# Six of sixteen row-block pairs of a feed-forward product done with seven block products in place of eight

## The chip, the cores and the metric

One core of a Trainium2 chip runs one program. The metric is the device time in microseconds, the median of several executions. The kernel before takes 1193.26 us.

## The reference

The input x has 4 x 1024 rows of 1024 numbers: 32 blocks ("tiles") of 128 rows. Three stages follow one another; each adds to x. The change touches the first.

```python
def ffn(x):                       # stages 1 and 3; x is the layer-normed input
    dots = softmax(x @ centroids.T / 0.1)          # 64 clusters
    hits = dots > 0.01
    dense = x @ weight.T + bias                    # weight 1024 x 1024
    return where(any(hits, axis=1)[:, None] & any(hits, axis=0)[assignments][None, :], dense, 0)
x = x + 0.5 * ffn(layernorm(x))
x = x + attention(layernorm(x))   # projections of q, k, v; attention over the 32 channels of a head
x = x + 0.5 * ffn(layernorm(x))
```

## The kernel before

All is float32. A product is made from three: each operand is split into a rounded high part and the rest (`w_hi`, `w_lo`; `even_hi`, `even_lo` for even pairs and `odd_hi`, `odd_lo` for odd pairs), and `product` (line 280) runs, for each of 8 blocks of the contraction, hi x hi, hi x lo and lo x hi into one bank of 512 columns: 24 matmuls. W is transposed and split at the start, in 16 steps (`transpose_rows`, `high_rows`, `low_rows`).

The first stage goes over the tiles in pairs p = 0 to 15 (tiles 2p and 2p+1). A tile t goes through these steps, each on its own engine:

- SP loads x (`load_first`, line 396, three buffers `xa`), VectorE takes mean and variance (`stats_first`), Pool makes the factors (`factors_first`, line 628), ScalarE the normed rows (`norm_first`, line 742).
- From tile 4 on, SP stores the normed rows (`store_normed`) and loads them back with their 32 x 32 blocks in transposed places, as four transfers (`load_blocks`, line 410); VectorE turns each block (`turn_first`, line 984). Tiles 0 to 3 are turned by TensorE.
- ScalarE rounds the high part (`high_first`, line 751), VectorE subtracts for the low part (`low_first`, line 988). TensorE needs both.
- TensorE makes two products a tile, one for each half of the columns (`product_first(t, h)`, line 1273), and for each pair the cluster logits (`pair_first`, line 1293), which ScalarE copies (`copy_pair`, line 763) and TensorE turns (`fold_pair`, line 1302); VectorE and ScalarE make the softmax from them.
- VectorE adds the bias and moves a half from its bank to `f_out` (`read_first`, line 1000). A bank is free for its next product when this is done. Pool clears the rows not selected (`select_tokens`, line 631), SP stores `f_out[t % 2]` (`store_first`, line 425).

Beside it the projection weights are prepared, a block of 128 rows a pair from p = 1 on: SP loads `proj_raw` (`load_proj`), Pool sums heads (`sum_heads`), ScalarE moves k and v and rounds (`move_kv`, `high_proj`), Pool subtracts (`low_proj`).

Every engine runs its instructions strictly in the order in which they are written; a wait on a semaphore holds all that stands behind it. The orders are written by hand: lines 458 to 482 for SP's queue, 657 to 673 for Pool, 801 to 816 for ScalarE, 1057 to 1069 for VectorE and 1338 to 1347 for TensorE. There a pair is products (2p, 0) and (2p, 1), the logits of pair p+1, then (2p+1, 0) and (2p+1, 1); each product takes the bank that the product of the same half two tiles ago had:

```python
for p in range(1, NP - 2):
    product_first(2 * p, 0, {3 if p == 1 else 1: lambda: fold_pair(p)})
    product_first(2 * p, 1)
    if p > 1:
        pair_first(p + 1)
    product_first(2 * p + 1, 0)
```

## Time and profile before

| what | value |
|---|---|
| median of three runs | 1193.26 us (1192.64 to 1194.24) |
| the profiled execution, its own time | 1196.15 us |
| its span in the trace | 1194.3 us |
| busy: TensorE / VectorE / ScalarE / Pool | 1181.7 / 799.3 / 499.2 / 441.0 us |
| first stage, within the span | 0 to about 387 us |

Busy time is the time in which an engine had an instruction at work; a matmul's recorded length overlaps the next one's, so that the distance between starts tells the rate. The first stage is a third of the span. The durations below are those of this one execution.

### The profile page before, as it was taken

Reading aid. Unit: us, or ns where it says so; the run is one execution under the profiler, and the core shown is the slowest. Engines: PE = TensorE matmul, PEld = TensorE weight load, DVE = VectorE, ACT = ScalarE, POOL = GpSimd, SP = SyncE. Lnnn points to the kernel's source line nnn. Section 1 sums busy time; section 2 is a strip of 40 time slices with the busy share of each in tenths; the row PEclk is TensorE's granted clock in tenths of the full one; section 3 lists DMA queues with packets and bytes.
Section 4 is the critical chain, followed back from the end, with each engine's and each line's share of the span. In section 5 each row is a group of like instructions: output and inputs, shape, how many; then the busy total and the mean of one; then the engine's idle time right before and its main releaser. Section 6 shows DMA issues by size and latency. Waiting matters only on the chain.

```text
span 1194.3 us, 24986 instructions
## 1 busy us (share of the span) xinstructions
PE 1181.7 (99%) x10072; PEld 1002.5 (84%) x10072; DVE 799.3 (67%) x1272; ACT 499.2 (42%) x718; POOL 441.0 (37%) x582
## 2 busy tenths in 40 slices
PE   7999999999999999999999999999999999999998
PEld 6888888888888888888888888888888878888887
DVE  6654554455444477787777877778777774199987
ACT  5232233222211355656656656565565663211110
POOL 1335445543424643433434334344343210051332
PEclk9999999999999999999999999999999999999999
DMA  8578777876565366565565666565655565017885
GB/s 275 144 206 232 207 206 193 225 211 182 164 189 159 98 169 169 148 171 146 160 166 139 181 152 152 160 155 164 161 142 164 129 169 193 2 72 259 279 304 195
DMA packets 344978, 208.73 MB, mean 175 GB/s; under 512 B 289440, under 2 KB 308640, under 8 KB 344864
## 3 DMA queue, kind: packets, MB, share of 16 engines
q1 hardware_dynamic: 329696, 187.73, 56.2%
q10 hardware_dynamic: 15168, 19.40, 4.7%
q8 instruction: 80, 1.31, 0.5%
q14 instruction: 34, 0.28, 0.1%
HBM read 118.49 MB, written 88.60 MB: 173 GB/s over the span
## 4 chain that ended last, share of the span: by engine, by line
PE 91%; DMA 3%; DVE 2%; issue 1%; ACT 1%; SPq 1%; POOL 1%; POOLq 0%; DVEq 0%
PE ps_b L285 9%; PE ps_q L285 8%; PE ps_q L287 8%; PE ps_q L286 8%; PE ps_b L287 8%; PE ps_b L286 8%; PE ps_a L285 8%; PE ps_a L287 8%; PE ps_a L286 8%; PE ps_t L292 6%; PE ps_q L1450 3%; PE ps_q L299 2%; PE ps_q L301 2%; PE ps_q L1425 2%; DMA y_scratch<-xa 1%
## 5 line engine op out<-in xcount | busy, mean ns | idle before, releaser
L318 POOL TENSOR_TENSOR var_eps<-moments,eps 128x1 f32<-128x1 f32 x96 | 18.2, 190 | 396.6 <-DVE moments L314 396.6
L285 PE MATMUL ps_a<-w_hi,odd_hi 128*128 128x512 f32 x368 | 147.7, 401 | 0.0
L287 PE MATMUL ps_a<-w_hi,odd_lo 128*128 128x512 f32 x368 | 143.8, 391 | 0.0
L286 PE MATMUL ps_a<-w_lo,odd_hi 128*128 128x512 f32 x368 | 143.2, 389 | 0.0
L635 POOL TENSOR_SCALAR f_out<-f_out,token_on 128x1024 f32<-128x1024 f32 x30 | 85.6, 2852 | 75.6 <-DVE f_out L1013 75.3
L686 POOL TENSOR_TENSOR x_ring<-x_ring,f_tmp 128x1024 f32<-128x1024 f32 x32 | 77.3, 2414 | 91.2 <-DVE best L1159 58.5
L285 PE MATMUL ps_b<-proj_hi,y_hi 128*128 128x512 f32 x256 | 103.3, 403 | 0.0
L287 PE MATMUL ps_b<-proj_hi,y_lo 128*128 128x512 f32 x256 | 100.0, 391 | 0.0
L286 PE MATMUL ps_b<-proj_lo,y_hi 128*128 128x512 f32 x256 | 99.7, 390 | 0.0
L327 ACT ACTIVATE y_tok<-x_ring,norms 128x1024 f32<-128x1024 f32 x64 | 79.7, 1245 | 38.0 <-ACT o_head L881 21.0
L737 POOL TENSOR_TENSOR late<-late,mask 128x1024 f32<-128x1024 f32 x18 | 44.1, 2463 | 137.3 <-DMA late<-x_scratch 91.6
L1120 DVE TENSOR_TENSOR y_lo<-ps_t,y_hi 128x1024 fp32r<-128x1024 f32 x32 | 39.2, 1224 | 76.1 <-ACT y_hi L900 76.1
L893 ACT COPY v_diag<-part 32x256 f32<-32x256 f32 x128 | 82.7, 646 | 1.1
L287 PEld LDWEIGHTS ps_a<-w_hi,odd_lo 128*128 128x128 f32 x368 | 69.1, 188 | 15.1
L286 PEld LDWEIGHTS ps_a<-w_lo,odd_hi 128*128 128x128 f32 x368 | 69.3, 188 | 13.1
L285 PEld LDWEIGHTS ps_a<-w_hi,odd_hi 128*128 128x128 f32 x368 | 69.2, 188 | 12.7
L285 PE MATMUL ps_q<-w_hi,odd_hi 128*128 128x512 f32 (+1 forms) x208 | 79.5, 382 | 0.0
L287 PE MATMUL ps_q<-w_hi,odd_lo 128*128 128x512 f32 (+1 forms) x208 | 79.3, 381 | 0.0
L286 PE MATMUL ps_q<-w_lo,odd_hi 128*128 128x512 f32 (+1 forms) x208 | 79.3, 381 | 0.0
L285 PE MATMUL ps_q<-proj_hi,y_hi 128*128 128x256 f32 x256 | 74.8, 292 | 0.0
L287 PE MATMUL ps_q<-proj_hi,y_lo 128*128 128x256 f32 x256 | 72.5, 283 | 0.0
L286 PE MATMUL ps_q<-proj_lo,y_hi 128*128 128x256 f32 x256 | 72.4, 283 | 0.0
(219 smaller groups left out, 3113.1 us busy)
## 6 DMA issues: line engine op xcount, KB each, us to landing
xa<-in_L_attn_x SPq DMA_DIRECT2D x32, 512.0 KB, 5.0
f_tmp<-f_scratch SPq DMA_DIRECT2D x32, 512.0 KB, 4.2
x_ring<-in_L_attn_x SPq DMA_DIRECT2D x32, 512.0 KB, 3.6
f_scratch<-f_out SPq DMA_DIRECT2D x30, 512.0 KB, 4.0
x_scratch<-x_ring SPq DMA_DIRECT2D x30, 512.0 KB, 3.5
y_scratch<-xa SPq DMA_DIRECT2D x28, 512.0 KB, 4.6
ya_tok<-y_scratch SPq DMA_DIRECT2D x112, 128.0 KB, 3.3
late<-x_scratch SPq DMA_DIRECT2D x22, 512.0 KB, 6.7
```

What stands on the lines that cost most here:

```text
L285: pe.matmul(acc, hi[:, k, :], w_h[:, k, cols], start=(k == 0), stop=False)
L286: pe.matmul(acc, hi[:, k, :], w_l[:, k, cols], start=False, stop=False)
L287: last = pe.matmul(acc, lo[:, k, :], w_h[:, k, cols], start=False, stop=(k == KB - 1))
L292: last = pe.transpose(ps_t[:, k, :], src[:, k * P:(k + 1) * P], ident[:, :])
L299: last = pe.matmul(pair_ps, cen[:, k, :], hi[:, k, :, :], start=(k == 0), stop=(k == KB - 1))
L327: return act.activation(y, x, ACT.Identity, bias=norms[of][:, t, 0:1], scale=norms[of][:, t, 1:2])
L635: pool.tensor_scalar(f_out[t % 2][:, :], f_out[t % 2][:, :], token_on[0][:, t:t + 1], None, ALU.mult).then_inc(f1_on, 1)
L686: pool.tensor_tensor(x_ring[t % RING][:, :], x_ring[t % RING][:, :], f_tmp[:, :], ALU.add).then_inc(x1, 1)
L737: pool.tensor_tensor(f[:, :], f[:, :], mask[:, :], ALU.mult).then_inc(s_masked, 1)
L893: last = act.copy(v_diag[rows, :].rearrange("p (k q g c) -> p q k g c", k=R4, g=HKV, c=T4)[:, :, :, :, c], v_cols[rows, :].rearrange("p (q ...
L1120: dve.tensor_tensor(y2_lo[:, :, :], ps_t[:, :, :], y2_hi[:, :, :].bitcast(F32), ALU.subtract).then_inc(lo2, 1)
L1450: last = pe.matmul(scores_of[32 * c:32 * c + 32, r, :, j, :], q_head[rows, n * D:(n + 1) * D], k_mask[rows, n * P:(n + 1) * P].rearrange(" ...
```

## The change

Pairs 4 to 9 (`SEVEN`) are computed with seven products of half the contraction (12 matmuls each) in place of eight such halves. The operands are cut in two by rows (the two tiles of the pair), by contraction and by columns. Pool makes four sums of the input's blocks in place (`sum_blocks`), ScalarE and VectorE split them (`high_sum`, `low_sum`) into `odd_hi` and `odd_lo`; all six pairs have their own input in `even_hi` and `even_lo`. VectorE combines the seven results by eight reads; Pool adds the difference of the two bias halves (`bias_first`). The selection of these tiles moves from Pool to ScalarE (`select_first`).

Four combinations of W's blocks are made once, during pairs 1 to 3, through one buffer `t_sum`: VectorE sums (3, 3, 2 and 2 instructions of 2048 columns, in `blocks_three`, `blocks_one`, `blocks_two`, `blocks_four`), ScalarE rounds, Pool subtracts (the last one VectorE). Three go to `t_hi` and `t_lo`, the fourth over a quarter of W, which is stored in memory before and loaded back after the last pair. `t_sum` lies where the odd pairs' normed rows go later (`ya_more`), and `t_hi`, `t_lo` where the projection weights go: these are now prepared from pair 10 on, two blocks a pair. Pair 3 has its products by halves of the columns. Some semaphores that are done by then are used again under new names (`t_step`, `t_hi_set`, `t_lo_set`, `block_step`, `seven_done`). The core of the diff:

```diff
+SA, SB = 4, 10
...
+t_hi = middle.enter_context(nc.sbuf_tensor("t_hi", [P, 3, QB, HALF], F32R))
+t_lo = middle.enter_context(nc.sbuf_tensor("t_lo", [P, 3, QB, HALF], F32R))
...
         if t - 2 < BY_PE:
             sp.wait_ge(t1, t - 1)
+        elif p == SA + 1:
+            sp.wait_ge(t_lo_set, 5)
+        elif SA + 1 < p <= SB:
+            sp.wait_ge(lo1, t - 3)
+            sp.wait_ge(sum_lo, parts_count(p - 2, 4))
         else:
             sp.wait_ge(lo1, t - 1)
+        if SA < p <= SB:
+            sp.wait_ge(y_in[t % 2], 64 * ((t - BY_PE) // 2))
...
-        sp.wait_ge(f1_on, t + 1)
+        sp.wait_ge(f1_on, t + 2 - 2 * (t % 2) if t // 2 in SEVEN else t + 1)
...
         if p > 0:
             store_first(2 * p - 1)
+        if p - 1 in SEVEN:
+            store_first(2 * p - 2)
+        if p > SB:
+            load_next_proj(2 * (p - SB) - 1)
+        if p == NP - 2:
+            load_next_proj(KB)
         if 2 * p + 5 < LAST:
             load_first(2 * p + 5)
         if 2 * p + 4 < NT:
             load_first(2 * p + 6)
         if p == NP - 2:
             load_attention()
-        store_first(2 * p)
+        if p not in SEVEN:
+            store_first(2 * p)
         if 2 * p + 5 < LAST:
             store_normed(2 * p + 5)
         if 2 * p + 7 == LAST:
             load_first(LAST)
-        if 1 <= p <= KB:
-            load_proj(p - 1, [w[(p - 1) * P:p * P].rearrange("p d h -> p (d h)") for w in (Wq, Wk, Wv)])
-        if p == KB + 1:
-            load_proj(KB, [b.rearrange("d h -> (d h)").partition_broadcast(P) for b in (bq, bk, bv)])
+        if SB <= p < NP - 2:
+            load_next_proj(2 * (p - SB))
         if 2 * p + 5 < NT:
             load_blocks(2 * p + 5)
+        if p == 1:
+            sp.wait_ge(wt_lo, 2 * KB)
+            for n, w in enumerate((w_hi, w_lo)):
+                sp.dma_start(w_d[n], upper(w)[:, :, half(1)].bitcast(F32)).then_inc(w_saved, 16)
+        if p == SB - 1:
+            sp.wait_ge(seven_done, seven_count(p, 1))
+            for n, w in enumerate((w_hi, w_lo)):
+                sp.dma_start(upper(w)[:, :, half(1)].bitcast(F32), w_d[n]).then_inc(w_back, 16)
...
+    def low_block(m):
+        n = T_ORDER[m]
+        pool.wait_ge(t_hi_set, m + 2)
+        pool.tensor_tensor(t_lo[:, n], t_sum[:, :, :], t_hi[:, n].bitcast(F32),
+                           ALU.subtract).then_inc(t_lo_set, 1)
+    def sum_blocks(p):
+        top, bottom = first_turned(2 * p), first_turned(2 * p + 1)
+        pool.wait_ge(lo1, 2 * p + 2)
+        pool.tensor_tensor(lower(bottom), upper(bottom), lower(bottom), ALU.add).then_inc(sum_set, 1)
+        pool.tensor_tensor(upper(bottom), upper(top), upper(bottom), ALU.subtract).then_inc(sum_set, 1)
+        pool.wait_ge(sum_set, sums_count(p, 2))
+        pool.tensor_tensor(upper(top), lower(bottom), upper(top), ALU.subtract).then_inc(sum_set, 1)
+        pool.wait_ge(sum_set, sums_count(p, 3))
+        pool.tensor_tensor(lower(top), lower(top), upper(top), ALU.subtract).then_inc(sum_set, 1)
+    def bias_first(p):
+        pool.wait_ge(block_step, block_count(p, 3))
+        if p == SA:
+            pool.wait_ge(t_step, 2 + 11)
+        pool.tensor_tensor(f_out[0][:, half(1)], f_out[0][:, half(1)], bias_diff[:, :], ALU.add).then_inc(bias_step, 1)
+        pool.wait_ge(f1_read[0], 2 * p + 2)
+        pool.tensor_tensor(f_out[1][:, half(1)], f_out[1][:, half(1)], bias_diff[:, :], ALU.add).then_inc(bias_step, 1)
...
+        if p in SEVEN:
+            sum_blocks(p)
+            if p == SA:
+                select_tokens(2 * p - 1)
+            factors_first(2 * p + 4)
+            bias_first(p)
+            factors_first(2 * p + 5)
+            continue
+        if p > 0 and p != SB:
             select_tokens(2 * p - 1)
+        if p == SB:
+            pool.wait_ge(f1_on, 2 * SB)
         if 2 * p + 4 < NT:
             factors_first(2 * p + 4)
         if 2 * p + 5 < NT:
             factors_first(2 * p + 5)
+        if 2 <= p < SA:
+            low_block((p - 2) * 2)
+        if p > SB:
+            sum_heads(2 * (p - SB) - 1)
+            low_proj(2 * (p - SB) - 1)
         select_tokens(2 * p)
-        if 2 <= p < KB + 2:
-            sum_heads(p - 2)
-            low_proj(p - 2)
-        if p == KB + 2:
-            sum_heads(KB)
-        if p == KB + 3:
-            pool.wait_ge(kv_moved, KB + 1)
-            pool.wait_ge(q_summed, KB + 1)
-            pool.memset(v_diag[:, :], 0.0).then_inc(zeroed, 1)
+        if p == 2:
+            low_block(1)
+        if p >= SB:
+            sum_heads(2 * (p - SB))
+            if 2 * (p - SB) < KB:
+                low_proj(2 * (p - SB))
...
+    def high_block(m):
+        act.wait_ge(t_step, 2 + (3, 6, 8, 10)[m])
+        if m < 3:
+            act.copy(t_hi[:, T_ORDER[m]], t_sum[:, :, :]).then_inc(t_hi_set, 1)
+        else:
+            act.wait_ge(ffn1[1], 2 * SA)
+            act.wait_ge(w_saved, 48)
+            act.copy(upper(w_hi)[:, :, half(1)], t_sum[:, :, :]).then_inc(t_hi_set, 1)
+    def high_sum(p, n):
+        act.wait_ge(sum_set, sums_count(p, n + 1))
+        if n == 2 and p == SA:
+            for h in range(2):
+                act.wait_ge(ffn1[h], 2 * SA)
+        elif n == 2:
+            act.wait_ge(seven_done, seven_count(p - 1, 7))
+        act.copy(sum_at(odd_hi, n), sum_rows(p, n)).then_inc(sum_hi, 1)
+    def select_first(t):
+        p = t // 2
+        act.wait_ge(on_set, p + 1)
+        if t % 2:
+            act.wait_ge(f1_on, 2 * p)
+            act.wait_ge(f1_read[0], 2 * p + 2)
+            act.wait_ge(f1_read[1], 2 * p + 1)
+        else:
+            act.wait_ge(f1_read[0], 2 * p + 1)
+            act.wait_ge(f1_read[1], 2 * p + 2)
+        act.activation(f_out[t % 2][:, :], f_out[t % 2][:, :], ACT.Identity,
+                       scale=token_on[0][:, t:t + 1]).then_inc(f1_on, 1)
...
+        if p - 1 in SEVEN:
+            select_first(2 * p - 2)
+        if p in SEVEN:
+            high_sum(p, 2)
+            copy_pair(p)
+            high_sum(p, 1)
+            high_sum(p, 0)
+            pair_soft_exp(act, p)
+            high_sum(p, 3)
+            norm_first(2 * p + 4)
+            high_first(2 * p + 2)
+            high_first(2 * p + 3)
+            norm_first(2 * p + 5)
+            select_first(2 * p + 1)
+            continue
+        if p == SB:
+            copy_pair(p)
         high_first(2 * p + 2)
         if p == 0:
             norm_first(2 * p + 4)
         pair_soft_exp(act, p)
-        if p == 0:
-            high_first(2 * p + 3)
-        else:
-            high_first(2 * p + 3)
+        high_first(2 * p + 3)
+        if p > 0:
             norm_first(2 * p + 4)
         norm_first(2 * p + 5)
-        if 2 <= p < KB + 3:
-            move_kv(p - 2)
-        if 2 <= p < KB + 2:
-            high_proj(p - 2)
-        copy_pair(p + 1)
+        if p > SB:
+            move_kv(2 * (p - SB) - 1)
+            high_proj(2 * (p - SB) - 1)
+        if 1 <= p < SA - 1:
+            high_block(p - 1)
+        if p == SA - 1:
+            high_block(2)
+            high_block(3)
+        if p >= SB:
+            move_kv(2 * (p - SB))
+            high_proj(2 * (p - SB))
+        if p + 1 not in SEVEN:
+            copy_pair(p + 1)
     high_first(NT - 2)
     pair_soft_exp(act, NP - 2)
     high_first(LAST)
+    move_kv(KB - 1)
+    high_proj(KB - 1)
+    move_kv(KB)
     copy_pair(NP - 1)
...
+    def blocks_three():
+        dve.wait_ge(wt_lo, 2 * KB)
+        dve.wait_ge(onehot_set, 1)
+        t_combine(t_sum[:, :, :], LOWER_HI[:, :, half(1)], UPPER_HI[:, :, half(1)], ALU.subtract)
+        t_combine(t_sum[:, :, :], t_sum[:, :, :], LOWER_LO[:, :, half(1)], ALU.add, 1)
+        t_combine(t_sum[:, :, :], t_sum[:, :, :], UPPER_LO[:, :, half(1)], ALU.subtract, 2)
+    def blocks_one():
+        dve.wait_ge(t_lo_set, 2)
+        t_combine(t_sum[:, :, :], UPPER_HI[:, :, half(1)], UPPER_HI[:, :, half(0)], ALU.subtract)
+        t_combine(t_sum[:, :, :], t_sum[:, :, :], UPPER_LO[:, :, half(1)], ALU.add, 4)
+        t_combine(t_sum[:, :, :], t_sum[:, :, :], UPPER_LO[:, :, half(0)], ALU.subtract, 5)
...
+    def low_block_four():
+        at = (slice(None), slice(0, QB), half(1))
+        dve.wait_ge(t_hi_set, 5)
+        dve.wait_ge(t_lo_set, 4)
+        dve.tensor_tensor(w_lo[at], t_sum[:, :, :], w_hi[at].bitcast(F32), ALU.subtract).then_inc(t_lo_set, 1)
...
+    def top_one(p):
+        dve.wait_ge(seven_done, seven_count(p, 2))
+        dve.wait_ge(f1_stored[0], 16 * p)
+        dve.tensor_tensor(TOP[0], ps_a[:, :], bias_a[:, half(0)], ALU.add).then_inc(block_step, 1)
...
+        if p == SA:
+            read_first(2 * p - 1, 0)
+        elif p - 1 in SEVEN:
+            top_right(p - 1)
+        else:
+            read_first(2 * p - 1, 1)
+        if p in SEVEN:
+            stats_first(2 * p + 4)
+            low_sum(p, 2)
+            low_sum(p, 1)
+            pair_soft_in(dve, p)
+            low_sum(p, 0)
+            low_sum(p, 3)
+            pair_soft_out(dve, 0, p)
+            top_one(p)
+            turn_first(2 * p + 2)
+            top_two(p)
+            turn_first(2 * p + 3)
+            top_left(p)
+            low_first(2 * p + 2)
+            low_first(2 * p + 3)
+            bottom_three(p)
+            bottom_left(p)
+            stats_first(2 * p + 5)
+            top_five(p)
+            bottom_right(p)
+            continue
         turn_first(2 * p + 2)
         pair_soft_in(dve, p)
         low_first(2 * p + 2)
         pair_soft_out(dve, 0, p)
         stats_first(2 * p + 4)
         turn_first(2 * p + 3)
-        read_first(2 * p, 0)
+        if p != SA - 1:
+            read_first(2 * p, 0)
         low_first(2 * p + 3)
         stats_first(2 * p + 5)
-        read_first(2 * p, 1)
-        read_first(2 * p + 1, 0)
+        if p == 2:
+            blocks_one()
+        if p == SB:
+            read_first(2 * p + 1, 0)
+            read_first(2 * p, 1)
+        elif p == SA - 1:
+            blocks_four()
+            read_first(2 * p, 1)
+            read_first(2 * p + 1, 1)
+            low_block_four()
+            read_first(2 * p, 0)
+        else:
+            if p == 1:
+                blocks_three()
+            read_first(2 * p, 1)
+            if p == 2:
+                blocks_two()
+            read_first(2 * p + 1, 0)
...
+        block_product(acc_b[1], x22, w4)
+        if p == SA:
+            pe.wait_ge(f1_read[0], 2 * SA - 1)
+        else:
+            pe.wait_ge(block_step, block_count(p - 1, 1))
+        block_product(ps_a[:, :], x11, w11, {1: lambda: fold_pair(p)})
+        pe.wait_ge(sum_lo, parts_count(p, 1))
+        if p == SA:
+            pe.wait_ge(f1_read[0], 2 * SA)
+        else:
+            pe.wait_ge(block_step, block_count(p - 1, 2))
+        block_product(ps_b[:, :], s2, w2)
+        if p > SA:
+            pe.wait_ge(f1_read[0], 2 * p - 1)
+        block_product(t_banks[0], x12, w21)
...
+        pe.wait_ge(sum_lo, parts_count(p, 4))
+        block_product(t_banks[1], s4, w22)
...
+        if p in SEVEN or p == SB:
+            pair_first(p)
+        if p in SEVEN:
+            pair_products(p)
+            continue
+        if p == SA - 1:
+            product_first(2 * p, 1, {1: lambda: fold_pair(p)})
+            product_first(2 * p + 1, 1)
+            product_first(2 * p, 0)
+            product_first(2 * p + 1, 0)
+            continue
+        product_first(2 * p, 0, {3 if p in (1, SB) else 1: lambda: fold_pair(p)})
+        if p == SB:
+            product_first(2 * p + 1, 0)
+            product_first(2 * p, 1)
+            pair_first(p + 1)
+            product_first(2 * p + 1, 1)
+            continue
         product_first(2 * p, 1)
         if p > 1:
```

## Rows read from the trace of the kernel before

**Rows 1.** The page: busy time, clock by slice, chain by engine.
```profile
PE 1181.7 (99%) x10072; PEld 1002.5 (84%) x10072; DVE 799.3 (67%) x1272; ACT 499.2 (42%) x718; POOL 441.0 (37%) x582
...
PEclk9999999999999999999999999999999999999999
...
PE 91%; DMA 3%; DVE 2%; issue 1%; ACT 1%; SPq 1%; POOL 1%; POOLq 0%; DVEq 0%
```

**Rows 2.** Timeline of TensorE, pair 7: start us, us, engine, line, what.
```profile
194.78 0.39 PE L285 MATMUL ps_a<-w_hi,odd_hi 128*128 128x512 f32 x1
195.01 0.39 PE L286 MATMUL ps_a<-w_lo,odd_hi 128*128 128x512 f32 x1
```

**Rows 3.** Timeline of TensorE: logits of pair 3, first matmuls of pairs 3 and 4.
```profile
83.89 0.38 PE L299 MATMUL ps_q<-odd_hi,cen 128*128 128x256 f32 x1 [1.07 <-DVE odd_lo L991]
...
96.78 0.39 PE L285 MATMUL ps_a<-w_hi,odd_hi 128*128 128x512 f32 x1
...
120.71 0.39 PE L285 MATMUL ps_a<-w_hi,even_hi 128*128 128x512 f32 x1
```

**Rows 4.** Groups by line of VectorE, 100 to 340 us: xcount, busy us, mean ns, idle before.
```profile
L986 DVE STREAM_TRANSPOSE ya_tok<-ya_tok 128x1024 f32<-128x1024 f32 x20 | 24.3, 1216 | 0.3 <-DMA ya_tok<-y_scratch 0.3
L310 DVE BATCH_NORM_STATS2 bn<-xa 128x6 f32<-128x512 f32 x20 | 13.7, 686 | 0.0
...
L991 DVE TENSOR_TENSOR even_lo<-ya_tok,even_hi 128x1024 fp32r<-128x1024 f32 x11 | 13.5, 1225 | 2.7 <-ACT even_hi L755 2.7
...
L1013 DVE TENSOR_TENSOR f_out<-ps_b,bias_a 128x512 f32<-128x512 f32 x10 | 6.9, 691 | 59.0 <-PE ps_b L287 59.0
```

**Rows 5.** Groups by line of ScalarE, 100 to 340 us.
```profile
L327 ACT ACTIVATE xa<-xa,norms 128x1024 f32<-128x1024 f32 x20 | 24.9, 1243 | 28.4 <-POOL norms L323 28.4
L755 ACT CAST odd_hi<-ya_tok 128x1024 fp32r<-128x1024 f32 x10 | 10.5, 1055 | 60.2 <-DVE ya_tok L986 60.2
```

**Rows 6.** Groups by line of Pool, whole span.
```profile
L635 POOL TENSOR_SCALAR f_out<-f_out,token_on 128x1024 f32<-128x1024 f32 x30 | 85.6, 2852 | 75.6 <-DVE f_out L1013 75.3 <-issue 0.3
L686 POOL TENSOR_TENSOR x_ring<-x_ring,f_tmp 128x1024 f32<-128x1024 f32 x32 | 77.3, 2414 | 91.2 <-DVE best L1159 58.5 <-DMA x_ring<-in_L_attn_x 32.2
...
L652 POOL TENSOR_TENSOR proj_lo<-proj_sum,proj_hi 128x768 fp32r<-128x768 f32 x8 | 14.8, 1844 | 7.6 <-ACT proj_hi L779 7.6
```

**Rows 7.** Timeline of SP's queue, pair 7.
```profile
203.06 0.33 SPq L408 DMA_DIRECT2D y_scratch<-xa  x1
205.69 2.83 SPq L422 DMA_DIRECT2D ya_tok<-y_scratch  x4
...
209.79 0.43 SPq L427 DMA_DIRECT2D f_scratch<-f_out  x1
210.27 0.43 SPq L408 DMA_DIRECT2D y_scratch<-xa  x1
...
216.51 2.74 SPq L422 DMA_DIRECT2D ya_tok<-y_scratch  x4
```

**Rows 8.** Timeline of VectorE: end of tile 7's statistics, turn of tile 7.
```profile
63.07 0.67 DVE L1013 TENSOR_TENSOR f_out<-ps_q,bias_a 128x512 f32<-128x512 f32 x1
...
80.24 1.25 DVE L986 STREAM_TRANSPOSE ya_tok<-ya_tok 128x1024 f32<-128x1024 f32 x1 [1.51 <-DMA ya_tok<-y_scratch]
```

**Rows 9.** Busy time by stretch; the last three: clock, DMA share, GB/s.
```profile
190.00:192.00 2.00, 2.00 (x10) 1.69 (x9) 0.00 (x0) 0.00 (x0) 0.08 (x1) 1.00 1.02 415
```

**Rows 10.** The page, DMA issues: count, KB each, median us to landing.
```profile
xa<-in_L_attn_x SPq DMA_DIRECT2D x32, 512.0 KB, 5.0
...
f_scratch<-f_out SPq DMA_DIRECT2D x30, 512.0 KB, 4.0
```

**Rows 11.** Timeline of the last stage, Pool and VectorE.
```profile
1050.70 15.56 POOL L737 TENSOR_TENSOR late<-late,mask 128x1024 f32<-128x1024 f32 x6 [45.77 <-issue]
...
1061.08 3.17 DVE L1187 SCALAR_TENSOR_TENSOR late<-k_mask,token_on,late 128x1024 f32<-128x1024 f32 x1
...
1073.88 1.28 DVE L1187 SCALAR_TENSOR_TENSOR late<-k_mask,token_on,late 128x1024 f32<-128x1024 f32 x1
```

**Rows 12.** Last logits' copy, and the landing of the projection bias.
```profile
369.25 0.37 ACT L765 COPY pair_sums<-ps_q 128x256 f32<-128x256 f32 x1 [4.45 <-PE ps_q L299]
...
proj_raw<-in_L_attn_bq SPq DMA_DIRECT2D x1, 512.0 KB, 6.4
```

153 lines of the change are left out of this document (141 added, 12 removed).

## The prediction

> **What bounds the kernel now.** I read the page first: TensorE is busy 99% of the span, its granted clock is full throughout, and the chain that ended last lies on it for 91% [rows 1]. So only fewer matmuls, or a hole in front of one, can move the time. Then the timeline of TensorE: a 512-column matmul starts every 0.227 us, whatever its recorded 0.39 [rows 2]. Pairs start at 96.78 and 120.71: 23.93 us a pair, with one hole before, 1.1 us at 83.89 [rows 3]. The other engines' rows give the durations that must fit under that: VectorE [rows 4], ScalarE [rows 5], Pool [rows 6], and the queue of SP [rows 7].
>
> **The gain.** A pair falls from 96 matmuls to 7 x 12 = 84: 12 x 0.227 = 2.7 us, six pairs 16.3 us, all on the path. A pair could then take 21.2 us. The logits' products and their folding stay.
>
> **What the pair needs elsewhere.** VectorE gains four differences and four more reads at 0.61 apart (durations 0.69), in all 17.5 us of the 21.2; Pool's six adds of 512 columns are 1.25 each (1024 take 2.41, 768 1.84 [rows 6]). Work fits; order decides.
>
> **Step 1, preparing the weight blocks (pairs 1 to 3), times on the old trace's axis.** All four sums share `t_sum`: VectorE sums, ScalarE rounds, Pool subtracts, and only then may VectorE go on. No row has 2048 columns; bounds are 2 and 4 times the 1024-column row, less the fixed part. I take 2.3 us on VectorE (0.69 at 512, 1.22 at 1024), 2.0 on ScalarE (1.05 at 1024 [rows 5]), 4.7 on Pool. Work alone: VectorE 7 + 7 + 4.7 + 4.7, ScalarE 4 x 2, Pool 3 x 4.7, last difference 2.3: 48 us, from 63.1 [rows 8], against 57.6 until 120.7. But each link stands in a queue:
> - `blocks_three`, 63.1 to 70.1, is ahead of the read of (2, half 1). Pool's selection (2.85 [rows 6]) of tile 2 ends at 73.6, its store is 5.6 late, the store and load of normed tile 7 stand behind it on SP; its blocks land at 82.9, where the turn was at 80.2 [rows 8]. Logits of pair 3 wait until 86.4: 2.6 us more.
> - The saved half of W, 2 x 1 MB, takes 5 us at the 415 GB/s that a full queue shows [rows 9], in front of x of tile 9, which lands about 92. `low_block(0)` is behind that tile's factors: 94.7 to 99.4. `blocks_one` ends at 106.4, ahead of the read of (4, half 1); the first product of pair 3, now (6, half 1), wants that bank at 99.2: 7.9 us. The rounding stands ahead of `copy_pair(3)`: 1.0 more.
> - `low_block(1)` is behind the selection of tile 4, which needs that read: 110 to 114.7; `blocks_two` to 119.4; reads of (5, 0) and (5, 1) to 120.6, and (7, half 1) wants the last at 113.8: 6.8 us.
> - TensorE is done with pair 3 and the logits of pair 4 at 138.9. `high_block(2)` is behind the norms of tiles 10 and 11 (136.0), `low_block(2)` to 140.7, `blocks_four` 145.4, rounding 147.4, last difference 149.8. The first of the seven starts at 149.8, not 120.7: **29.1 us**, the sum of these waits. Its ends: 20 (W's save costs nothing, norms early) and 35.
> - Pool then selects tile 6 (read at 150.4) until 153.3, three sums until 157.2, ScalarE rounds, then copies the logits at 158.1; the fold in the second product wants them at 153.2: **4.9 us** (2 to 5).
>
> **Step 2, the pair loop.** `load_blocks` of an odd tile now stands ahead of the two stores of selected rows, and `top_one` waits for the second. From `top_one`: VectorE until `bottom_three` 7.0, Pool's two bias adds 2.5, factors 1.1, norm 1.25: 12.0. Store of y to issue of the blocks 2.6 (203.06 to 205.69). Behind the blocks issued at 205.69 came x, f_out, y; the y was in at 216.5, 10.8 later; one 512 KB transfer is 1.26 us, so a second in line lands after 9.5 [rows 7]. Loop: 12.0 + 2.6 + 9.5 = 24.1 us, against 21.2. The lag reaches TensorE through `bottom_three`, bias adds, factors, sums, `copy_pair`, fold: slack uses the first 1.5 us, then 0.9, 3.9, 2.9, 2.9, 2.9: **13.5 us** over pairs 5 to 9. With landings 3 us sooner the loop is 21.1 and costs nothing; 1.5 us later it costs 20.
> SP's own queue: the page has stores of f_out at 4.0 and x at 5.0 to landing [rows 10]; in the seven-product pairs no projection load shares it. Before them SP stands at the blocks of tile 10 until the last difference (149.8), with x of tile 12 and the stores of tiles 6 and 7 behind it: x lands at 157.7, in front of the first `low_sum`, which the lag above already holds.
>
> **A rule against the change.** In the last stage VectorE instructions with two SBUF inputs take 3.17 us while Pool multiplies two tiles, 1.28 when it doesn't [rows 11]; both kinds are what is added. The fourth sum of a pair and the first `low_sum` meet, at most 0.6 us a pair, off the store loop: 0 in the sum, 4 at the upper end. (The Trainium skill, GPSIMD Engine Reference, Specifications, says that Pool's SBUF interfaces are shared with VectorE and contended by instructions with two SBUF inputs; the trace agrees. Taken as full serialization of all four differences it would add 2.8 us a pair.)
>
> **Step 3, leaving.** `copy_pair(10)` is behind norm and two selections on ScalarE: fold 3.4 us late. W's half is loaded behind the last odd blocks: 300.7 to about 312.8 on a chain where product (20, 1) is due 309.9: 2.9. **6.3 us** (1 to 10).
>
> **Step 4, projections moved behind pair 10.** Two a pair: 1.5 us for the odd blocks pushed late (0 to 4). At the end ScalarE waits for the bias rows before `copy_pair(15)`: `move_kv(7)` needs the last high copy (367.4), only then SP issues the biases, landing 6.4 after issue; the copy is at 377.3, it was at 369.25 [rows 12]: **7.0 us** after the fold's slack (4 to 9). The selections of pairs 4 to 9, moved from Pool to ScalarE, I cost at nothing (1.2 a tile [rows 5], before the store loop's own wait ends); without that cover they are 2.4 us a pair, 12 in all.
>
> **Sum.** 29.1 + 4.9 - 16.3 + 13.5 + 6.3 + 1.5 + 7.0 = +46.0, on the profiled 1196.15 us (span 1194.3) 1242; that execution is 2.9 above the median of the runs, 1193.26, so I forecast **1239**. Slower, by nearly 4%.
>
> **Rivals.**
> - *The covers hold (faster).* Places: the `t_sum` chain and the store loop. If the chain stayed within 57.6 us of its 48 and the loop under 21.2, 1193.3 - 16.3 = 1177. For it: the work does fit. Against: every link has a named predecessor in a queue. It decides once the weight blocks cost less than 16.3. Chance 0.07.
> - *Only the preparation is exposed.* Landings 3 us sooner, exits short: 29.1 + 4.9 - 16.3 + 3 = +21, 1214. For it: stores alone land in 4.0. Chance 0.24.
> - *The clock falls in the long holes.* The trace has no hole past 2 us at which to see it; its clock is 2.4 GHz throughout. At 1.2 GHz a product of 24 takes 5.4 more. The holes before 149.8 lie in front of further waits and absorb it; the one at fold 4 and the last don't: 2 x 5.4, 1250. Chance 0.08. (The Trainium skill, TensorE: Matmul & The Clock Gate, part on the clock gate, has idling send the array to half rate; no row here shows it.)
> - *Near nothing*, the preparation at its lower end less all the rest: within 0.2% of 1193, chance 0.03.
> - The forecast itself 0.58. That the seven products are not what runs is excluded by the order of TensorE's calls.
>
> **Numbers.** A measurement can tell 0.2%, some 2.4 us. Ends added: low 20 + 2 - 16.3 + 0 + 1 + 0 + 4 = +11; high 35 + 5 - 16.3 + 20 + 10 + 4 + 9 = +67. All ends at once are unlikely; 8 in 10 is 1208 to 1260, which takes in the second and third rival. Faster 0.08, same 0.02, slower 0.90.
>
> **What would show it.** In the profile of after: the first w_hi product into ps_q's second bank for pair 4 about 29 us late; TensorE holes near 7 to 11 us on `f_out` and `w_lo` between 99 and 150; pairs 5 to 9 at 24, not 21.2; VectorE idle at `top_one` on the store of f_out; at the end `pair_sums` late behind `proj_bias`. Wrong, if pairs run at 21.2 with no holes, or if the first of the seven starts within 10 us of 120.7.

## The result, and the profile after

The kernel after takes 1288.01 us (four runs, 1285.61 to 1290.28), against 1193.04 in the same session (1192.64 to 1194.24): a ratio of 1.0794, interval 1.0771 to 1.0817. The forecast was 1239, range 1208 to 1260. The direction was right; the size was missed by 49 us, and the result lies outside the range. The profiled execution took 1289.05 us, span 1287.2. All of the loss lies in the first stage: its last transposes start at 480.88 us, where they started at 387.65, which is 93.2 later.

The page of the kernel after, its lines for busy time, clock and chain, as in [rows 1]:

```profile
PE 1190.3 (92%) x10000; PEld 1005.0 (78%) x10000; DVE 856.8 (67%) x1332; ACT 531.3 (41%) x758; POOL 476.1 (37%) x609
...
PEclk9988799999888889999999999999999999999999
...
PE 60%; DMA 11%; DVE 10%; POOL 9%; SPq 4%; issue 4%; ACT 2%; POOLq 0%; DVEq 0%; ACTq 0%
```

TensorE holds 60% of the chain where it held 91%, and the clock, full in every slice before, stands at seven or eight tenths in eight of the first stage's fifteen slices. The timeline of TensorE in the kernel after, the matmuls that stand behind a hole (start, duration, then what; in brackets the idle time before it and who ended it; a hole, counted from start to start less 0.227, is up to 0.2 us longer):

```profile
85.31 0.58 PE L354 MATMUL ps_q<-odd_hi,cen 128*128 128x256 f32 x1 [2.89 <-DVE odd_lo L1177]
...
105.37 0.77 PE L340 MATMUL ps_q<-w_hi,odd_hi 128*128 128x512 f32 x1 [4.32 <-DVE f_out L1199]
...
118.79 0.76 PE L340 MATMUL ps_q<-w_hi,odd_hi 128*128 128x512 f32 x1 [4.47 <-DVE f_out L1199]
...
147.81 0.80 PE L1614 MATMUL ps_q<-w_hi,even_hi 128*128 128x512 f32 x1 [9.10 <-DVE w_lo L1237]
...
156.17 0.69 PE L361 MATMUL ps_q<-ident,pair_sums 128*128 128x128 f32 x2 [2.42 <-ACT pair_sums L923]
...
203.87 0.69 PE L361 MATMUL ps_q<-ident,pair_sums 128*128 128x128 f32 x2 [3.42 <-ACT pair_sums L923]
...
308.34 0.47 PE L340 MATMUL ps_q<-w_hi,even_hi 128*128 128x512 f32 x1 [3.90 <-DMA w_lo<-w_scratch]
...
330.23 0.69 PE L361 MATMUL ps_q<-ident,pair_sums 128*128 128x128 f32 x2 [6.51 <-ACT pair_sums L923]
...
363.10 0.69 PE L361 MATMUL ps_q<-ident,pair_sums 128*128 128x128 f32 x2 [7.19 <-ACT pair_sums L923]
...
398.61 0.69 PE L361 MATMUL ps_q<-ident,pair_sums 128*128 128x128 f32 x2 [9.25 <-ACT pair_sums L923]
...
429.46 0.69 PE L361 MATMUL ps_q<-ident,pair_sums 128*128 128x128 f32 x2 [10.64 <-ACT pair_sums L923]
...
458.88 0.69 PE L361 MATMUL ps_q<-ident,pair_sums 128*128 128x128 f32 x2 [13.38 <-ACT pair_sums L923]
```

The first four are the preparation, at the places and for the reasons that Step 1 gave. The last five are the folds of pairs 11 to 15, after the seven-product pairs are over: 6.5, 7.2, 9.25, 10.6 and 13.4, together **47.0 us**, where Step 4 had 8.5. The folds of pairs 6 to 10 wait 3.4, 0.9, 1.2, 1.7 and 1.5.

There is a second cost. TensorE's timeline behind the fold of pair 12, and the busy time by stretch (the three last columns: granted clock, DMA share, GB/s):

```profile
364.43 0.63 PE L342 MATMUL ps_a<-w_hi,even_lo 128*128 128x512 f32 x1
364.86 0.63 PE L340 MATMUL ps_a<-w_hi,even_hi 128*128 128x512 f32 x1
```
```profile
160.00:300.00 140.00, 131.27 (x619) 108.66 (x618) 106.73 (x197) 55.45 (x71) 56.37 (x78) 0.99 0.69 180
...
450.00:480.00 30.00, 20.13 (x78) 15.29 (x78) 6.57 (x19) 3.84 (x7) 14.55 (x14) 0.78 0.39 149
```

Starts are 0.43 us apart instead of the 0.227 of [rows 2], and the granted clock from 364 to 366 us is 0.50: the array runs at 1.2 GHz for some microseconds. In this kernel twelve such stretches follow the twelve holes of 2.4 us idle or more; none follows the holes of 1.9 or less. Adding up, over the matmuls of the stage from 60 us on (before that the two kernels are within 0.4 us of each other), what each start is late against the full clock's spacing: holes 87.5 us, half clock 24.6, the rest 1.9. The same sum over the trace of before is 1.2, 0.9 and 1.7. So 110.2 us were added, the seven products gave 16.3, and the difference of 93.9 is the 93.2 measured, within 1 us. This says where TensorE's time went. It does not say that full clock would give 24.6 back: where other engines alone set the end of the next wait, a slow TensorE only makes that wait shorter (more on this below).

### The profile page after: what moved, and what is told of

It reads as the page before. It is cut to its first block, busy times and chain, and to the rows that moved or that the text cites. A ratio compares the mean times of both kernels' runs of the same rounds, so it can differ in the third digit from the quotient of the medians.

```text
span 1287.2 us, 25003 instructions
## 1 busy us (share of the span) xinstructions
PE 1190.3 (92%) x10000; PEld 1005.0 (78%) x10000; DVE 856.8 (67%) x1332; ACT 531.3 (41%) x758; POOL 476.1 (37%) x609
## 4 chain that ended last, share of the span: by engine, by line
PE 60%; DMA 11%; DVE 10%; POOL 9%; SPq 4%; issue 4%; ACT 2%; POOLq 0%; DVEq 0%; ACTq 0%
PE ps_b L340 6%; PE ps_b L342 6%; PE ps_b L341 6%; PE ps_a L340 5%; PE ps_a L342 5%; PE ps_a L341 5%; PE ps_t L347 5%; PE ps_q L340 4%; PE ps_q L342 4%; PE ps_q L341 4%; PE ps_q L1830 2%; POOL f_out L718 2%; DMA y_scratch<-xa 2%; SPq L485 2%; DMA xa<-in_L_attn_x 2%
## 5 line engine op out<-in xcount | busy, mean ns | idle before, releaser
L373 POOL TENSOR_TENSOR var_eps<-moments,eps 128x1 f32<-128x1 f32 x96 | 22.3, 232 | 369.2 <-DVE moments L369 369.2
L340 PE MATMUL ps_a<-w_hi,odd_hi 128*128 128x512 f32 x344 | 139.4, 405 | 0.0
L342 PE MATMUL ps_a<-w_hi,odd_lo 128*128 128x512 f32 x344 | 135.4, 394 | 0.0
L341 PE MATMUL ps_a<-w_lo,odd_hi 128*128 128x512 f32 x344 | 135.0, 392 | 0.0
L382 ACT ACTIVATE y_tok<-x_ring,norms 128x1024 f32<-128x1024 f32 x64 | 79.7, 1245 | 41.5 <-ACT o_head L1067 20.7
L342 PEld LDWEIGHTS ps_a<-w_hi,odd_lo 128*128 128x128 f32 x344 | 65.2, 189 | 14.3
L341 PEld LDWEIGHTS ps_a<-w_lo,odd_hi 128*128 128x128 f32 x344 | 65.6, 191 | 12.5
L340 PE MATMUL ps_q<-w_hi,odd_hi 128*128 128x512 f32 (+1 forms) x160 | 63.7, 398 | 8.8 <-DVE f_out L1199 8.8
L802 POOL TENSOR_TENSOR f_tmp<-f_tmp,mask 128x1024 f32<-128x1024 f32 x32 | 68.8, 2150 | 2.5 <-DMA f_tmp<-f_scratch 2.5
L361 PE MATMUL ps_q<-ident,pair_sums 128*128 128x128 f32 x64 | 15.0, 321 | 58.1 <-ACT pair_sums L923 58.1
L718 POOL TENSOR_SCALAR f_out<-f_out,token_on 128x1024 f32<-128x1024 f32 x18 | 51.3, 2849 | 46.5 <-DVE f_out L1199 46.5
```

Source lines behind the costliest of these rows:

```text
L340: pe.matmul(acc, hi[:, k, :], w_h[:, k, cols], start=(k == 0), stop=False)
L341: pe.matmul(acc, hi[:, k, :], w_l[:, k, cols], start=False, stop=False)
L342: last = pe.matmul(acc, lo[:, k, :], w_h[:, k, cols], start=False, stop=(k == KB - 1))
L382: return act.activation(y, x, ACT.Identity, bias=norms[of][:, t, 0:1], scale=norms[of][:, t, 1:2])
L718: pool.tensor_scalar(f_out[t % 2][:, :], f_out[t % 2][:, :], token_on[0][:, t:t + 1], None, ALU.mult).then_inc(f1_on, 1)
L802: pool.tensor_tensor(f_tmp[:, :], f_tmp[:, :], mask[:, :], ALU.mult).then_inc(f_masked, 1)
```

## The experiments

All times are compared with runs of the kernel before in the same session (1195.4 to 1196.6 there), so the ratio is what counts; a step of 0.001 is 1.2 us. Experiments change the kernel after unless another is named.

| kernel | median us | ratio (interval) | against after, us |
|---|---|---|---|
| after | 1288.01 | 1.0794 (1.0771 to 1.0817) | |
| copy first | 1287.12 | 1.0772 (1.0751 to 1.0793) | -3 |
| stores | 1280.79 | 1.0720 (1.0702 to 1.0738) | -9 |
| preparation | 1271.84 | 1.0647 (1.0627 to 1.0666) | -18 |
| restore earlier | 1288.18 | 1.0787 (1.0766 to 1.0808) | -1 |
| loads first | 1260.96 | 1.0548 (1.0532 to 1.0564) | -29 |
| loads first, copy first | 1253.32 | 1.0482 (1.0460 to 1.0504) | -37 |
| one load only | 1259.03 | 1.0516 (1.0498 to 1.0535) | -33 |
| most changes | 1229.48 | 1.0284 (1.0257 to 1.0311) | -61 |
| two buffers | 1222.38 | 1.0212 (1.0193 to 1.0231) | -70 |
| all | 1214.83 | 1.0157 (1.0137 to 1.0177) | -76 |
| before, with held holes | 1261.75 | 1.0553 (1.0537 to 1.0568) | |

### The logits' copy ahead of the moves (copy first)

```diff
+                    if p + 1 not in SEVEN:
+                        copy_pair(p + 1)
                     if p >= SB:
                         move_kv(2 * (p - SB))
                         high_proj(2 * (p - SB))
-                    if p + 1 not in SEVEN:
-                        copy_pair(p + 1)
```

The last copy, `copy_pair(NP - 1)`, and the exponentials behind it likewise go ahead of `move_kv(KB)`.

> The changed kernel with one reordering on ScalarE: from pair 10 on, the copy of the next pair's logits stands ahead of the even projection block's moves (and the last copy ahead of the bias rows' move). Nothing else moves; the two blocks a pair are still loaded, summed, moved and rounded. Theory A (the 47 us of holes at the folds of pairs 11 to 15 are the logits' copy waiting in ScalarE's queue behind a block that has not landed): these five holes shrink to under 2 us each, the half-clock stretches behind them go too (about 8 us), and the time is 1230 to 1242, 46 to 58 below the changed kernel's 1288. Rival B (the loop through Pool, the store, the loads and the moves takes longer than a pair whatever stands behind it, so the wait moves to the normed rows or to the next copy, which still stands behind the odd block's moves): holes of the same total come elsewhere, 1270 to 1288. Rival C (in between: the odd block's move, ahead of the copy, takes over as the wait): 1245 to 1270, with ScalarE waiting for the odd block's landing right before the copy.

Measured: 3 us less, which the intervals don't tell from nothing. Theory A falls, B holds. The folds of pairs 11 to 14 don't wait any more, but the logits do, in the timeline of TensorE of this kernel:

```profile
342.87 0.58 PE L354 MATMUL ps_q<-even_hi,cen 128*128 128x256 f32 x1 [8.41 <-DVE even_lo L1177]
...
379.62 0.58 PE L354 MATMUL ps_q<-odd_hi,cen 128*128 128x256 f32 x1 [10.39 <-DVE odd_lo L1177]
```

The holes of the tail are 8.6, 10.5, 11.2, 5.5 and 8.1, 43.9 in all. The copy's place in the queue decided only where the hole shows. Something with a period longer than a pair feeds all of it.

Back in the trace of the kernel after, that something can be followed. ScalarE, one block's move to the next but one, 32.9 us apart:

```profile
326.49 1.08 ACT L930 COPY proj_sum<-proj_raw 128x256 f32<-128x256 f32 x2 [9.88 <-DMA proj_raw<-in_L_attn_Wv]
...
329.81 0.36 ACT L923 COPY pair_sums<-ps_q 128x256 f32<-128x256 f32 x1
...
359.37 1.07 ACT L930 COPY proj_sum<-proj_raw 128x256 f32<-128x256 f32 x2 [11.66 <-DMA proj_raw<-in_L_attn_Wv]
...
362.68 0.36 ACT L923 COPY pair_sums<-ps_q 128x256 f32<-128x256 f32 x1
```

Pool, its subtraction for the block and the selection behind it, twice:

```profile
329.98 1.82 POOL L759 TENSOR_TENSOR proj_lo<-proj_sum,proj_hi 128x768 fp32r<-128x768 f32 x1 [0.94 <-ACT proj_hi L939]
331.78 2.85 POOL L718 TENSOR_SCALAR f_out<-f_out,token_on 128x1024 f32<-128x1024 f32 x1
...
347.79 1.84 POOL L759 TENSOR_TENSOR proj_lo<-proj_sum,proj_hi 128x768 fp32r<-128x768 f32 x1 [0.94 <-ACT proj_hi L939]
349.61 2.86 POOL L718 TENSOR_SCALAR f_out<-f_out,token_on 128x1024 f32<-128x1024 f32 x1
```

SP's queue:

```profile
334.65 0.34 SPq L490 DMA_DIRECT2D f_scratch<-f_out  x1
335.09 0.38 SPq L506 DMA_DIRECT2D proj_raw<-in_L_attn_Wq  x1
...
352.49 0.33 SPq L490 DMA_DIRECT2D f_scratch<-f_out  x1
...
353.39 0.73 SPq L506 DMA_DIRECT2D proj_raw<-in_L_attn_Wq  x1
```

A ring closes: the block lands (326.5), Pool sums it and subtracts (to 331.8), the selection stands behind (to 334.6), the store waits for the selection, the next block's loads stand behind the store (335.1), they land, and round again (349.6, 352.5, 353.4) until the next landing at 359.4. No engine is full in it: from 320 to 480 us Pool is busy for 71.2 us of 160, ScalarE for 35.7. TensorE has no part in it either: from 326.5 to 429.0 no selection on Pool waits for a read of a bank. (The selection at 439.33 does, for 8.3 us, and the one at 465.70 for 11.8.) A block costs half of 32.9, 16.4 us. By this reckoning one block a pair, as before the change, fits under 23.9, and two don't.

### The loads of the blocks ahead of the stores (loads first)

```diff
                 for p in range(NP - 1):
+                    if p > SB:
+                        load_next_proj(2 * (p - SB) - 1)
                     if p > 0:
                         store_first(2 * p - 1)
...
+                    if SB <= p < NP - 2:
+                        load_next_proj(2 * (p - SB))
                     if p not in SEVEN:
                         store_first(2 * p)
```

The two calls are taken out where they stood.

> The changed kernel with two moves in SP's queue from pair 10 on: the loads of the odd projection block are issued ahead of the store of the previous odd tile, and those of the even block ahead of the store of the even tile. ScalarE's and Pool's orders stay. Theory D (pairs 11 to 15 run at the length of a ring: block landed, Pool's three sums and its subtraction, the selection behind them, the store that waits for the selection, the next block's loads behind the store, landing; twice a pair, 32.9 us from one even block's move to the next): each of the two load issues comes about 6 us earlier, the ring falls by about 12 to 21 us and the pairs run at TensorE's pace again. The five holes of 47 us fall below 12, the half-clock stretches behind them go, and the time is 1232 to 1245. Rival E (Pool's or ScalarE's own work for two blocks a pair is the bound): the holes stay above 30 and the time above 1270. Rival F (the loads themselves, two of 768 KB a pair beside the other transfers, are slow): the landing takes as much longer as the issue is earlier, and the time stays above 1270.

Measured: 29 us less, the largest gain of one edit, with ScalarE and Pool in their old order. The tail's holes fall from 47.0 to 20.5 (4.0, 2.0, 7.5, 7.0). Rivals E and F fall as the main cause; of D, which said under 12 and 1232 to 1245, the mechanism holds and the size doesn't. What is left of ScalarE's waits, first for the block, then for Pool's sum, in this kernel's list of waits (total us, times, longest; the kernel after had 57.6, 5, 14.0 and 8.2, 8, 1.5 in these lines):

```profile
ACT proj_sum L930 <- DMA proj_raw<-in_L_attn_Wv: 25.4, 4, 7.1
ACT proj_hi L939 <- POOL proj_sum L755: 13.2, 8, 6.4
```

### Both (loads first, copy first)

> Both reorderings, the loads of the projection blocks ahead of the stores on SP and the logits' copy ahead of the even block's moves on ScalarE. Theory D: with the ring shorter than TensorE's pair, what is left of the holes is the copy's place in ScalarE's queue, so this is as fast as the loads alone or up to 8 us faster, 1226 to 1242. Rival E or F: the holes stay, at other places of the pair, above 1265.

Measured: 8 us less than the loads alone, the upper end of what was expected of the step, though from 1261 and not from 1240, so that the time is above the range expected. The copy's place, worth nothing while the ring set the pace, is worth 8 us once it doesn't. The tail's holes are 14.5 us.

### Only the first block loaded (one load only)

```diff
+                    if k > 0:
+                        return
                     for src, a, b in zip(srcs, (0, EMB, EMB + HD), (EMB, EMB + HD, EMB + 2 * HD)):
...
-                    pool.wait_ge(raw_in, 48 * k + 48)
+                    pool.wait_ge(raw_in, 48)
```

The wait in `move_kv` is changed in the same way.

> The changed kernel with only the first of the nine projection blocks loaded; the other eight (24 transfers) are left out and their sums, moves, roundings and subtractions run at once on the first one's data. The queries, keys and values are wrong by that. It asks how much of the tail is the wait for landings, with every instruction of ScalarE and Pool in its place. Theory D (the ring of landings and stores): without the landings the ring has nothing left to wait for, and the folds of pairs 11 to 15 wait less than 8 us together; 1226 to 1238. Rival (the two engines' own work for two blocks a pair and the selection behind it hold the copy of the logits): more than 20 us of holes stay, above 1250.

Measured: 33 us less. The landings of eight blocks, which this kernel leaves out, were worth 29 us of holes: 17.6 are left, between what the theory (under 8) and the rival (over 20) had, and the time is the rival's. Of the 17.6, 7.1 are the first block's landing, which this kernel keeps. The rest is the part of the rival that is true. ScalarE, then Pool, at the fold of pair 14:

```profile
408.53 0.83 ACT L941 CAST proj_hi<-proj_sum 128x768 fp32r<-128x768 f32 x1 [4.14 <-POOL proj_sum L757]
409.27 0.36 ACT L925 COPY pair_sums<-ps_q 128x256 f32<-128x256 f32 x1
```
```profile
403.20 2.85 POOL L720 TENSOR_SCALAR f_out<-f_out,token_on 128x1024 f32<-128x1024 f32 x1
406.02 0.63 POOL L753 TENSOR_TENSOR proj_sum<-proj_raw 128x256 f32<-128x256 f32 x1
```

The block's sum stands behind a selection of 2.85 us on Pool, ScalarE's rounding waits for the sum, and the copy stands behind the rounding: a wait that no transfer is in.

### The stores ahead of the block loads (stores)

```diff
                     if p - 1 in SEVEN:
                         store_first(2 * p - 2)
+                        load_blocks(2 * p + 3)
...
-                    if 2 * p + 5 < NT:
+                    if 2 * p + 5 < NT and p not in SEVEN:
                         load_blocks(2 * p + 5)
```

> The changed kernel with SP's queue reordered in the seven pairs: both stores of the selected rows are issued before the next odd tile's four block transfers are waited for, so that the even half-buffer of the next pair is free earlier. Theory (the period of the seven pairs is set by the second store behind the block loads): the period falls from 22.8 to about 21.2 to 21.6, the holes at the folds of pairs 6 to 10 (3.4, 0.9, 1.2, 1.7, 1.5) go, and the time falls by 8 to 11 to 1277 to 1280. Rival (the block loads, now issued later, become the wait: the turned rows come late and the sums with them): no gain or a loss of up to 6, 1286 to 1294, with TensorE waiting for the odd sums instead of the f_out read.

Measured: 9 us less, 1 us above the range of the theory. The folds of pairs 5 to 10 no longer wait; the mechanism of Step 2 holds. Part of the gain is lost again where the ring begins: the fold of pair 11 waits 8.7 us idle in place of 6.5.

### The preparation requeued (preparation)

The edits, in the order of the pairs: SP saves the quarter of W in pair 2 instead of 1 and issues x of tile 12 ahead of the blocks of tile 10; Pool makes `low_block(0)` ahead of the factors and `low_block(2)` between them; ScalarE makes `high_block` behind `copy_pair`, and `high_block(2)` behind the exponentials. On VectorE:

```diff
-                    if p == 2:
-                        blocks_one()
...
-                        blocks_four()
                         read_first(2 * p, 1)
                         read_first(2 * p + 1, 1)
+                        blocks_four()
...
-                        if p == 1:
-                            blocks_three()
                         read_first(2 * p, 1)
                         if p == 2:
-                            blocks_two()
+                            blocks_one()
                         read_first(2 * p + 1, 0)
+                        if p == 1:
+                            blocks_three()
```

`blocks_two` goes to pair 3, behind `pair_soft_out`.

> The changed kernel with the preparation of the four weight blocks requeued in pairs 1 to 3 and nothing left out: reads of the banks stand ahead of the VectorE block sums, Pool's subtractions ahead of the factors, ScalarE's rounding behind the logits' copy, and the save of the quarter of W one pair later. Theory (the preparation's 27 us are queue positions, not the engines' work): the first product of the seven starts at 122 to 128 in place of 147.8, and the time falls by 22 to 32 with the half-clock stretches that follow the holes, to 1256 to 1266. Rival (the chain of sum, rounding and subtraction through the one buffer is itself too long for pairs 1 to 3: 10 sums of 2.3, three subtractions of 4.6 and their waits): the start falls by less than 10, 1278 to 1286, with TensorE waiting for w_lo or t_lo at the first of seven.

Measured: 18 us less. The first of the seven starts at 131.06, 16.8 earlier, with 6.1 us of waiting left; the two holes on `f_out` are gone. The theory is right in kind; the start came 3 us later than its upper end, and the gain is 4 short of its lower end.

### The quarter of W restored earlier (restore earlier)

`w_back`'s two transfers are issued right behind `load_first(2 * p + 6)` in pair 9.

> The changed kernel with the two transfers that restore the quarter of W issued one step earlier in SP's queue, ahead of the last stores and loads of pair 9. Theory (the hole of 3.9 us before the first whole product of pair 10 is queue position): the hole goes, with the half-clock stretch behind it, 1282 to 1285. Rival (the transfers wait for the seventh product anyway, and what stands behind them is late in its place): within 1.5 us of the changed kernel's 1288.

Measured: nothing that can be told (-1 us). The hole of 3.9 us did go, but the one at the fold of pair 11 is 10.0 instead of 6.5. The fold itself starts at 329.70, where it was at 330.23: TensorE only arrives earlier at the next wait, which ends when the first projection block has landed and been rounded. The time is the rival's.

### Most of it together (most changes)

> The loads ahead of the stores, the copy ahead of the moves, both stores of the seven pairs ahead of the block loads, and the preparation requeued, all in one kernel. Theory D says that the tail's ring took back part of what the preparation and the stores gave by themselves, so that with the ring gone they add up in full: 50 for the tail with its clock, 24 for the preparation's holes, 7 for the stores off 1288 leave 1203 to 1214, still above the kernel before, since holes at the folds of the seven pairs and the wait for the restored quarter stay. Rival (each fix only moves the wait): above 1225.

Measured: 61 us less, 1229.5. The parts alone gave 37, 18 and 9, 64 in all: they add to within 3 us. The sum that the theory reached, with more for the preparation and the tail, is missed; but the rival, whose number came, is wrong as well, since no fix only moved its wait. Still the seven products show what they give. TensorE's timeline, folds of pairs 5 and 6 of this kernel:

```profile
162.87 0.38 PE L361 MATMUL ps_q<-ident,pair_sums 128*128 128x128 f32 x2
...
184.09 0.38 PE L361 MATMUL ps_q<-ident,pair_sums 128*128 128x128 f32 x2
```

From there to 247.71 four pairs take 21.2 us each without a hole, against 23.93 [rows 3]. One delay was new, here and in the kernel with the preparation requeued. VectorE, then Pool:

```profile
115.68 4.62 DVE L1183 TENSOR_TENSOR even_lo<-ya_tok,even_hi 128x1024 fp32r<-128x1024 f32 x1 [1.12 <-ACT even_hi L887]
```
```profile
114.61 4.62 POOL L727 TENSOR_TENSOR t_lo<-t_sum,t_hi 128x2048 fp32r<-128x2048 f32 x1
```

A subtraction that takes 1.225 [rows 4] took 4.62; it ended 1.07 after Pool's, as if it had only then begun. Behind it VectorE works without a break until 128.1, and the rounding and the last difference, for which TensorE waits, stand at the end of that, so these 3.4 us are part of the 6.1 that the first of the seven still waited. (The Trainium skill, GPSIMD Engine Reference, Specifications, has Pool's SBUF interfaces shared with VectorE and contended by instructions with two SBUF inputs; the trace agrees.) In the kernel after, VectorE's instructions are stretched by about 4.8 us in all between 84 us and 482 us and Pool's by about 4.6, against the usual length of the same instruction, and by 0.9 us or less at any one place.

### A second buffer, and the last moves (two buffers, all)

The first gives blocks 1, 3 and 5 a buffer of their own, in what later is the end of `proj_lo`, so that `load_proj(k)` waits for block k-2 only; `move_kv` and `high_proj` of the even block go behind the next pair's exponentials, `low_proj` between the next factors, and the copy ahead of the odd block's moves.

> The most changed of the earlier kernels (loads ahead of stores, copy ahead of moves, stores of the seven pairs ahead of block loads, preparation requeued; 1229.5) with a second buffer for the projection blocks 1, 3 and 5, in the part of proj_lo that is filled last, and with the even block's moves and subtraction put off into the next pair, behind the softmax. Theory (the holes of 7.2, 2.5, 4.4 and 2.6 us in pairs 12 to 15 are ScalarE waiting for a block that could only be loaded once the one before was used up): they fall to under 5 together; 1214 to 1221. Rival (they come from the transfers' own queue, block loads of 3 to 10 us issue): above 1225.

The second:

```diff
+                def low_block_two():
+                    dve.wait_ge(t_hi_set, 4)
+                    dve.tensor_tensor(t_lo[:, T_ORDER[2]], t_sum[:, :, :], t_hi[:, T_ORDER[2]].bitcast(F32),
+                                      ALU.subtract).then_inc(t_lo_set, 1)
...
+                    if p == SA - 1:
+                        low_block_two()
                     low_first(2 * p + 3)
+                    if p == SA - 1:
+                        blocks_four()
```

with Pool's `low_block(2)` taken out, `high_block(3)` ahead of a norm, `copy_pair(4)` ahead of the first rounding, and the restore earlier.

> The kernel with two buffers, and three more moves: the last Pool subtraction of the preparation (4.6 us, during which a VectorE subtraction of 1.2 took 4.6 in the trace of the most changed kernel) is made by VectorE in 2.3; the fourth block's sums and rounding stand ahead of the reads and of a norm, and the first logits' copy of the seven ahead of a rounding; and the quarter of W is restored one step earlier. Theory: the first product of the seven starts at 125 to 128 in place of 131.8, the hole of 2.7 at the fold of pair 4 goes, and that of 3.9 at the logits of pair 11, where four block transfers stood behind the 2 MB of the restored quarter, goes too; 10 to 14 less than two buffers alone, 1202 to 1209, still above the kernel before. Rival (each only moves its wait): less than 5 below two buffers alone.

Measured: 1222.4 and 1214.8, 1 and 6 us above what was expected; the second step gave 7 to 8 us, between its theory and its rival. Two buffers take the tail's holes from 16.6 to 7.9, but 4.7 come up behind them, at the selection of hit clusters. With all moves VectorE's timeline has the difference at its own length again:

```profile
113.83 2.25 DVE L1250 TENSOR_TENSOR t_lo<-t_sum,t_hi 128x2048 fp32r<-128x2048 f32 x1
116.00 1.22 DVE L1198 TENSOR_TENSOR even_lo<-ya_tok,even_hi 128x1024 fp32r<-128x1024 f32 x1
```

and the first of the seven starts at 127.28. TensorE's waits in this kernel, 290 us to 420 us:

```profile
PE ps_q L363 <- DVE even_lo L1198: 9.5, 2, 5.5
PE ps_q L440 <- DVE hit L436: 4.9, 1, 4.9
```

The stage's account is 27.6 us of holes and 9.2 of half clock, less the 2.1 of before, so 34.7 lost against 16.3 gained; its end is 18.7 later than before. So no version here beats the kernel before. Whether another order of the tail would, was not tried.

### What a hole costs (before, with held holes)

```diff
+HELD = {5: 8, 7: 16, 9: 30, 11: 60, 13: 90}
...
+                    if p in HELD:
+                        for n in range(sum(HELD[c] for c in HELD if c < p), sum(HELD[c] for c in HELD if c <= p)):
+                            if n:
+                                pool.wait_ge(held, n)
+                            pool.memset(fill[:, :], 0.0).then_inc(held, 1)
...
+                    if p in HELD:
+                        pe.wait_ge(held, sum(HELD[c] for c in HELD if c <= p))
```

> The kernel before, with TensorE held at the start of pairs 5, 7, 9, 11 and 13 until Pool has written a small unused tile 8, 16, 30, 60 and 90 times, one write after the other: holes of rising length in a first stage that is otherwise unchanged. It measures what a hole costs beyond its own length. Theory (after a hole of more than about 2.6 us TensorE runs for about 2 us at half its rate, after shorter ones it does not): the longer holes are each followed by 8 to 14 matmuls at a spacing of 0.43 in place of 0.227, the time grows by the sum of the holes and by about 2 us for each long one, and nothing is made good later. Rival (the slack of the other engines makes good part of each hole, and the clock term is from something else): growth by less than the holes' sum, no half-clock stretches.

Measured: holes of 5.3, 6.7, 9.1, 14.4 and 19.6 us, 55.0 in all; the stage ends 67.0 later. (The hole at the logits of pair 3 grew as well, from 1.2 to 2.4.) Behind the longest, in TensorE's timeline:

```profile
401.42 0.79 PE L287 MATMUL ps_a<-w_hi,odd_hi 128*128 128x512 f32 x1 [19.45 <-POOL fill L666]
402.01 0.63 PE L288 MATMUL ps_a<-w_lo,odd_hi 128*128 128x512 f32 x1
402.44 0.63 PE L289 MATMUL ps_a<-w_hi,odd_lo 128*128 128x512 f32 x1
```

Half clock behind each of the five, 11.6 us more than in the trace of before, 2.3 a hole, with no relation to its length (the longest had 3.7 us of such a stretch, the shortest 5.3). Nothing was made good later: the theory holds for these lengths. Its limit of 2.6 us was not tested by them, since the shortest is twice that, and the natural holes of the other kernels speak against any such limit. Holes of 3.1 us idle (preparation, at 139.42, with a granted clock of 1.00 from 139 to 145 us; restore earlier, at 157.37) and of 3.3 (loads first and copy first, at 157.89) had no half clock behind them, and two of 1.9 did (loads first, at 379.69; restore earlier, at 294.96). (The Trainium skill, TensorE: Matmul & The Clock Gate, Part 1, has an idle array fall to half rate and work restore it; the trace agrees.)

## Why the prediction was wrong

**The gain, right.** 16.3 us: pairs of 21.2 us, as forecast, once nothing waits.

**Step 1, right.** Forecast 29.1 with the start of the seven at 149.8; measured 147.81, 27.1. The links were as long as taken: VectorE 2.3 (2.29 measured), Pool 4.7 (4.6). Its waits of 2.6, 7.9 and 1.0, 6.8 and 10.9 came out as 1.9 (3.05 less the 1.2 of before), 4.5, 4.6 and 9.1: 9 us shorter together, with 7 us of half clock between them. That the two nearly cancel is no luck. From 91.7 us on, the chain that ends the last wait runs through VectorE, ScalarE and Pool, and each wait on it is ended by one of them. VectorE's timeline in the kernel after:

```profile
97.67 2.29 DVE L1207 TENSOR_TENSOR t_sum<-w_hi 128x2048 f32<-128x2048 f32 x1 [5.77 <-POOL t_lo L724]
...
112.83 2.29 DVE L1207 TENSOR_TENSOR t_sum<-w_hi,t_sum 128x2048 f32<-128x2048 f32 x1 [7.61 <-POOL t_lo L724]
...
138.88 2.29 DVE L1207 TENSOR_TENSOR t_sum<-w_hi,t_sum 128x2048 f32<-128x2048 f32 x1 [8.97 <-POOL t_lo L724]
```

No read of a bank on it waits for TensorE, so a slower TensorE shortens the waits and leaves 147.81 where it is. The forecast had walked this chain (97.67 was forecast as 99.4, and the end stayed 2 us early). The fold of pair 4: 2.6, not 4.9. Requeueing took 17 us of the 27 away with no work removed, which shows that these were places in queues.

**Step 2, right in kind, too large.** 7.2 us over the folds of pairs 6 to 9 instead of 13.5, since the loop ran at 22.6 to 23.9 a pair rather than 24.1; the stores experiment confirms the loop by taking the holes away.

**Step 3, right in the sum.** 1.5 and 3.9, together 5.4, against 6.3; the parts had been forecast as 3.4 and 2.9.

**Step 4, wrong: the step that failed.** It put 1.5 us for "the odd blocks pushed late" and 7.0 at the end; 47.0 came. It named the wait at the end (the copy behind a block's landing on ScalarE) and gave it to the bias rows alone. The same wait stands in each of the pairs 11 to 15, because a ring of landing, sums, selection, store and next loads takes 16.4 us a block and was now to run twice in a pair of 23.9. (At the fold of pair 15 ScalarE does wait for the bias rows, 5.6 us at 457.55, but the ring had delayed them.) The step never walked that chain; for one block a pair the trace of before had no wait for a landing to show for it. Breaking the ring at SP gave 29 us, leaving out the landings 33. Moving the copy alone gave nothing.

**The clock, given 0.08 as a rival and nothing in the sum.** In TensorE's account it has 23.7 us. The rival had 5.4 us for each of two holes; twelve were followed by half clock, for 2.0 us each. So the single price was too high and the number of places far too low. Its thought that holes in a row absorb it did hold. The 7 us in front of 147.81 only shortened the waits there, as Step 1 shows, and the 5.4 behind the folds of pairs 11 to 13 stand in front of folds that the ring set. That leaves at most about 11 us as the clock's own cost; no run separates it. The prediction also said that the trace of before has no hole past 2 us at which to see the clock. It has one, at its very start. TensorE's timeline of before:

```profile
5.67 1.09 PE L1270 MATMUL ps_a<-ident,w_raw 128*128 128x128 f32 x4 [5.67 <-DMA w_raw<-in_L_ffn_weight]
...
10.28 1.47 PE L1270 MATMUL ps_q<-ident,w_raw 128*128 128x128 f32 x12
```

The matmuls of 128 columns start 0.213 us apart from 5.67 to about 10.1, behind 5.67 us without work, and 0.109 apart from 10.28 on. That is some 20 of them at half rate, about 2 us late in all, which is what a hole cost later. The granted clock reads 1.00 over this stretch; only the spacing shows it.

**The sum.** 27.1 + 2.6 - 16.3 + 7.2 + 5.4 + 47.0, 1.9 at the last transposes and 16.6 of half clock outside Step 1 make 91.5 of the 93.2 measured. Against the forecast of 46.0 the tail misses 38.5, the clock 16.6, and the other terms together give 9.6 back. These are the terms of TensorE's account; the 5.4 us of half clock that the ring covered would have come as holes at full clock, so that the ring's own share is nearer 44 us than 38.5.

**The rule on Pool and VectorE**, 0 with 4 at the upper end: right for this kernel, and 3.4 us as soon as the order changed.

## What to carry to other kernels

When work that ran beside a loop once a turn is compressed to twice a turn, add up its whole ring, landing to landing, through every queue that it passes, the stores among them; a ring that was hidden leaves no wait in the trace that would show its length. A reordering at the place where the wait shows moves the wait; find what has the period. And on a TensorE that never paused, price a new hole of some microseconds at its length plus about 2 us, where no wait that other engines set stands behind it; where one does, that wait takes the 2 us, and often the hole too, as in the kernel that restored the quarter of W earlier.

## What the runs showed of the hardware that was not expected

- The half-clock cost of a hole does not grow with it: 2.3 us on average for holes from 5.3 to 19.6 us, and 2.0 on average for the twelve of the kernel after, the shortest of which had TensorE idle for 2.42 us. Over all kernels, every hole of the first stage with more than 3.3 us idle was followed by half clock; between 1.8 and 3.3 some were and some were not.
- Pool and VectorE can hold each other up for as long as the other's instruction lasts. In the kernel with most changes a VectorE subtraction of 1.22 us became 4.62 beside a Pool subtraction of 4.62, and Pool's selection, 2.85 alone, took 4.96 beside VectorE's sums of 2048 columns.
